# Three edits to the first pass of a fused decoder block on one core: zero matmuls ahead of the inputs, the residual of half the inputs by identity matmuls, the value tile last

## What is computed

```python
w = (qw.astype(jnp.float32) - ZERO) * jnp.repeat(scales, GS, axis=0)   # groups of 128 channels
q, k, v = x @ w_q, x @ w_k, x @ w_v          # 32 query heads, 8 key and value heads, 128 wide
q, k = _apply_rope(q, cos, sin), _apply_rope(k, cos, sin)
attn = jax.nn.softmax(causal(q @ k.T / math.sqrt(HD)), axis=-1)
x = _layernorm(x + (attn @ v) @ w_o)
...
x = _layernorm(x + _L0_xattn_ref(x, ctx_4096, ...))
x = _layernorm(x + _L0_ffn_ref(x, ...))
```

## Time and profile before

| | us |
|---|---|
| time, median of 3 runs | 696.7 (695.96 to 698.34) |
| the profiled execution's own time | 701.41 |
| its span, first to last instruction | 699.6 |
| PE busy in the span | 641.2 (92%) |
| DVE busy | 561.9 (80%) |
| ACT busy | 463.5 (66%) |
| POOL busy | 421.1 (60%) |
| mean granted clock of PE | 0.976 of full speed |

### The profile page before, as it was taken

How to read it: one execution, slowest core, us unless ns; L and a number is a source line. 1 busy time by engine, 2 the same in 40 slices (tenths; PEclk the granted TensorE clock), 3 DMA queues, 4 the chain that set the end, 5 groups by cost and what they waited for, 6 DMA issues and landing times.

```text
span 699.6 us, 10934 instructions
## 1 busy us (share of the span) xinstructions
PE 641.2 (92%) x3271; PEld 449.2 (64%) x3272; DVE 561.9 (80%) x883; ACT 463.5 (66%) x1266; POOL 421.1 (60%) x370
## 2 busy tenths in 40 slices
PE   6588989999999999999999999999878998968994
PEld 4366767768778777787777877855544444457551
DVE  4967978989999999998899999963552968997446
ACT  5377959769798797887977979865624555523000
POOL 1558779889989989988998998871221000012002
PEclk9889999999999999999999999999989999999998
DMA  6564732341351252243234224230010000020003
GB/s 208 154 207 119 235 107 60 106 130 40 93 162 37 66 155 77 46 138 103 55 112 126 48 62 134 63 114 0 1 60 1 2 0 1 1 95 2 0 1 120
DMA packets 29611, 56.72 MB, mean 81 GB/s; under 512 B 4720, under 2 KB 4976, under 8 KB 29040
## 3 DMA queue, kind: packets, MB, share of 16 engines
q1 hardware_dynamic: 29552, 56.02, 28.2%
HBM read 32.93 MB, written 2.10 MB: 50 GB/s over the span
## 4 chain that ended last, share of the span: by engine, by line
PE 39%; DVE 8%; ACT 3%; POOL 2%; issue 2%; POOLq 0%; DVEq 0%; ACTq 0%
PE ps L1507 8%; PE ps L1446 8%; PE ps L1499 7%; PE ps L1725 4%; PE ps L1461 3%; PE ps L1487 3%; DVE arena L1305 2%; PE ps L1471 1%; ACT arena L959 1%; PE ps L1607 1%; DVE arena L1278 1%; DVE late L1272 1%; DVE w_area L1286 1%; PE ps L1716 1%; DVE y L1226 1%
## 5 line engine op out<-in xcount | busy, mean ns | idle before, releaser
L1074 DVE SCALAR_TENSOR_TENSOR arena<-ps,arena 128x512 f32<-128x512 f32 x288 | 212.7, 745 | 17.5 <-PE ps L1446 4.7
L1446 PE MATMUL ps<-x_hi,w_sb 128*128 128x512 f32 x384 | 175.3, 457 | 17.0 <-DVE arena L1074 8.1
L1446 PE MATMUL ps<-x_lo,w_sb 128*128 128x512 f32 x384 | 154.6, 403 | 0.0
L1102 DVE SCALAR_TENSOR_TENSOR y<-ps,arena,y 128x512 f32<-128x512 f32 x192 | 138.8, 744 | 14.9 <-PE ps L1499 10.7
L1499 PE MATMUL ps<-heads_hi,wo_sb 128*128 128x512 f32 x256 | 110.0, 430 | 6.9 <-DVE y L1102 5.3
L772 ACT ACTIVATE arena<-ps,small 128x128 f32<-128x128 f32 x256 | 90.9, 379 | 32.3 <-DVE small L1080 32.3
L597 POOL TENSOR_TENSOR arena<-arena,consts 128x512 f32<-128x512 f32 x75 | 97.0, 1293 | 22.8 <-DVE arena L1074 22.5
L603 POOL TENSOR_TENSOR arena<-arena,consts 128x512 f32<-128x512 f32 x75 | 96.9, 1292 | 20.6 <-DMA arena<-arena 19.2
L1446 PEld LDWEIGHTS ps<-x_hi,w_sb 128*128 128x128 f32 x384 | 74.5, 194 | 51.5 <-issue 11.2
L621 POOL TENSOR_TENSOR y<-arena,y 128x512 f32<-128x512 f32 x64 | 82.5, 1290 | 40.7 <-ACT arena L813 38.6
L1499 PE MATMUL ps<-heads_lo,wo_sb 128*128 128x512 f32 x256 | 101.8, 398 | 0.0
(11 more groups left out here) (130 smaller groups left out, 957.5 us busy)
## 6 DMA issues: line engine op xcount, KB each, us to landing
arena<-arena SPq DMA_DIRECT2D x160, 128.0 KB, 2.3
arena<-in_qkv SPq DMA_DIRECT2D x48, 256.0 KB, 4.1
arena<-in_o SPq DMA_DIRECT2D x32, 256.0 KB, 3.8
arena<-in_x_t SPq DMA_DIRECT2D x8, 256.0 KB, 3.5
y<-in_x SPq DMA_DIRECT2D x4, 512.0 KB, 4.4
arena<-in_ctx_t SPq DMA_DIRECT2D x4, 512.0 KB, 6.4
out<-y SPq DMA_DIRECT2D x8, 256.0 KB, 2.2
arena<-in_wk SPq DMA_DIRECT2D x1, 1024.0 KB, 5.0
```

What stands on the lines that cost most here:

```text
L1074: nc.vector.scalar_tensor_tensor(acc, group_bank(p, KC * c + g), scale_of(p // 2, c, g), acc, ALU.mult, ALU.add).then_inc(dve_scaled, 1)
L1102: nc.vector.scalar_tensor_tensor(dst, by_tile(out_bank(p, u)), out_scale_of(p // 2, u), dst, ALU.mult, ALU.add).then_inc(out_added, 1)
L1446: mm = nc.tensor.matmul(group_bank(p, u), w_sb[:, c, g, :], part[:, g, half * HALF:(half + 1) * HALF], start=(k == 0), stop=(k == 1))
```

## The change

- DVE's first instruction sets `mask_b` to zero, and PE multiplies it by itself eight times into bank 6 while it has no inputs (`stay_busy(8)`), and twice more ahead of group 0.3.
- The weight tiles are loaded, projected and summed in the order 0, 2, 3, 4, 5, 1 (`FIRST_TILES`). Six banks instead of seven hold the groups of pass 0, since bank 6 is used for the zeros and, with bank 5, for the new cuts. `place` gives a tile's position in the new order to all waits.
- `x_lo` of the second half is no longer made by DVE. PE makes it in PSUM as identity times the piece (in full float32) plus minus identity times `x_hi` (`cut_x` of PE), and ACT copies it to `x_lo` (`copy_x_lo`). PE does the four cuts after all 24 groups of pass 0, then `turn_v(0)`, which now waits for the last copy.
- SP: the two transfers of tile 2's turn stand between the second and the third piece of the second half. POOL: the cosine of tile 2 stands ahead of the sine of tile 0.
- In phase 0 alone, PE does `score(0)` ahead of groups 1.0 and 1.1, and DVE the first maximum ahead of the sum of 1.1.

```diff
+FIRST_TILES = [0, 2, 3, 4, 5, 1]
+FIRST_SUMS = "0.1 0.2 2.1 0.3 2.2 3.1 2.3 3.2 4.1 3.3 4.2 5.1 4.3 5.2 1.1 5.3 1.2 1.3".split()
...
-        first_ps = [0, 1, 2, 7, 3, 4, 6]
+        first_ps = [0, 1, 2, 7, 3, 4]
...
+        def x_cut_bank(g):
+
+            return banks[6 if g % 2 == 0 else 5]
...
             turn_first(0)
-            for g in range(KC):
-                load_x(1, g)
-            for c in ROPE_TILES[1:]:
+            load_x(1, 0)
+            load_x(1, 1)
+            turn_first(2)
+            load_x(1, 2)
+            load_x(1, 3)
+            for c in ROPE_TILES[2:]:
                 turn_first(c)
...
+            def copy_x_lo(g):
+                act.wait_ge(x_cut, g + 1)
+                nc.scalar.activation(x_lo[:, g, HALF:], x_cut_bank(g), ACT.Copy).then_inc(x_lo_ready, 1)
+
+            first_weights(2)
             scale_group(0, 0)
-            first_weights(2)
-            scale_group(0, 1)
-            act.wait_ge(consts_in, 16)
-            nc.scalar.activation(ident_b[:, :], ident, ACT.Copy).then_inc(mask_ready, 1)
             first_weights(3)
             scale_group(0, 2)
             first_weights(4)
+            act.wait_ge(consts_in, 16)
+            nc.scalar.activation(minus_ident[:, :], ident, ACT.Copy, scale=-1.0).then_inc(mask_ready, 1)
             scale_group(0, 3)
             first_weights(5)
+            nc.scalar.activation(ident_b[:, :], ident, ACT.Copy).then_inc(mask_ready, 1)
+            scale_group(0, 4)
+            first_weights(1)
+            cut_x(1, 0)
+            scale_group(0, 5)
+            cut_x(1, 1)
+            scale_group(0, 1)
+            cut_x(1, 2)
+            copy_x_lo(0)
+            cut_x(1, 3)
+            copy_x_lo(1)
+            nc.scalar.activation(mask_b[:, :, :], mask.unsqueeze(1).broadcast_to([P, QPK, P]), ACT.Copy).then_inc(mask_ready, 1)
+            copy_x_lo(2)
+            copy_x_lo(3)
             copy_v(0)
...
+            nc.vector.memset(mask_b[:, :, :], 0.0).then_inc(idle_ready, 1)
             for g in range(KC):
                 cut_x(0, g)
...
-            for name in FIRST_SUMS[:13]:
+            for name in FIRST_SUMS:
                 first_sum(name)
-            cut_x(1, 0)
-            first_sum("4.2")
-            first_sum("5.1")
-            cut_x(1, 1)
-            first_sum("4.3")
-            first_sum("5.2")
-            cut_x(1, 2)
-            first_sum("5.3")
             first_sin(3)
-            cut_x(1, 3)
             first_total(3)
...
             def turn_v(p):
                 wait(pe, dve_scaled, summed_count(p, 1))
                 wait_turn_bank(p - 1, "V")
+                if p == 0:
+                    wait(pe, x_lo_ready, 2 * KC)
...
                 groups(0, 3)
+                if f == 0:
+                    score(0)
                 groups(1, 0, 1)
-                score(0)
+                if f != 0:
+                    score(0)
...
-            for c in range(4):
+            def stay_busy(count):
+
+                for _ in range(count):
+                    nc.tensor.matmul(banks[6], mask_b[:, 0, :], mask_b[:, :, :].rearrange("p h k -> p (h k)"),
+                                     start=True, stop=True)
+
+            def cut_x(g):
+
+                pe.wait_ge(x_hi_ready, KC + g + 1)
+                wait(pe, x_lo_ready, KC + g - 1)
+                part = slice(HALF, T)
+                nc.tensor.matmul(x_cut_bank(g), ident, x_stage[:, g, part], start=True, stop=False)
+                nc.tensor.matmul(x_cut_bank(g), minus_ident[:, :], x_hi[:, g, part], start=False, stop=True).then_inc(x_cut, 1)
+
+            pe.wait_ge(idle_ready, 1)
+            stay_busy(8)
+            for g in range(3):
+                project(0, 0, g)
+            stay_busy(2)
+            project(0, 0, 3)
+            for c in FIRST_TILES[1:]:
                 for g in range(KC):
                     project(0, c, g)
             pe.wait_ge(consts_in, 16)
+            pe.wait_ge(mask_ready, 2)
+            for g in range(KC):
+                cut_x(g)
             turn_v(0)
-            for c in range(4, NT):
-                for g in range(KC):
-                    project(0, c, g)
-            pe.wait_ge(mask_ready, 2)
+            pe.wait_ge(mask_ready, 3)
             for f in range(LAST):
                 phase(f)
```

More of the change, by code:

```diff
@@ L376, in summed_count, with place, first_bank @@
             return scaled_count(p, c, KC - 1)
+        def place(p, c):
+            return FIRST_TILES.index(c) if p == 0 else c
         def product_bank(name):
             return product_ps[PRODUCTS.index(name) % 4]
+        def first_bank(u):
+            return first_ps[(KC * place(0, u // KC) + u % KC) % len(first_ps)]
         def group_bank(p, u):
             if p == 0:
-                return banks[first_ps[u % len(first_ps)]]
+                return banks[first_bank(u)]
             return product_bank(f"G{u}")
@@ L393, in wait_group_read @@
             if u % KC == 0:
-                wait(eng, act_scaled, NT * p + u // KC + 1)
+                wait(eng, act_scaled, NT * p + place(p, u // KC) + 1)
             else:
@@ L418, in wait_product_bank @@
             if f == -1:
-                u = int(name[1:]) - len(first_ps)
-                if u >= 0:
-                    wait_group_read(nc.tensor, 0, u)
+                u = int(name[1:])
+                before = KC * place(0, u // KC) + u % KC - len(first_ps)
+                if before >= 0:
+                    wait_group_read(nc.tensor, 0, KC * FIRST_TILES[before // KC] + before % KC)
                 return
@@ L439, in wait_product_bank @@
             bank = (0, 1, 2, 7)[PRODUCTS.index(name) % 4]
-            wait_group_read(nc.tensor, 0, max(u for u in range(GROUPS) if first_ps[u % len(first_ps)] == bank))
+            places = [KC * c + g for c in FIRST_TILES for g in range(KC)]
+            wait_group_read(nc.tensor, 0, [u for u in places if first_bank(u) == bank][-1])
         def att_bank(b):
             return banks[6 if b % 2 == 0 else 4]
+        def x_cut_bank(g):
+            return banks[6 if g % 2 == 0 else 5]
         def turn_y_bank(b):
@@ L494, in _ @@
             sp.dma_start(scales[:, :], t["qkv_scales"]).then_inc(scales_in, 16)
-            load_first_w(1)
             load_first_w(2)
+            load_first_w(3)
             sp.dma_start(consts[:, :, :], t["consts"]).then_inc(consts_in, 16)
-            for c in range(3, NT):
+            for c in FIRST_TILES[3:]:
                 load_first_w(c)
@@ L759, in scale_group @@
             def scale_group(p, c):
-                wait(act, group_done, GROUPS * p + KC * c + 1)
+                wait(act, group_done, GROUPS * p + KC * place(p, c) + 1)
                 wait_ring(act, p, c)
@@ L1066, in add_group @@
             def add_group(p, c, g):
-                wait(dve, group_done, GROUPS * p + KC * c + g + 1)
+                wait(dve, group_done, GROUPS * p + KC * place(p, c) + g + 1)
                 if g == 1:
-                    wait(dve, act_scaled, NT * p + c + 1)
+                    wait(dve, act_scaled, NT * p + place(p, c) + 1)
                 else:
@@ L1438, in project @@
                 if p % 2 == 0 and g == 0:
-                    wait(pe, w_ready, NT * (p // 2) + c + 1)
+                    wait(pe, w_ready, NT * (p // 2) + place(p, c) + 1)
                 if p < 2 and c == 0:
```

19 lines of the change are left out of this document (8 added, 11 removed).

## The result

| | before | after |
|---|---|---|
| time, median of 13 runs | 698.45 (695.96 to 701.49) | 692.06 (689.33 to 695.39) |
| ratio after/before, 95% interval | | 0.9907 (0.9887 to 0.9928) |
| profiled execution, its span | 701.41, 699.6 | 692.16, 690.4 |
| mean granted clock in it | 0.976 | 0.986 |

The change makes the kernel faster by 6.5 us, with 5.0 to 7.9 as the interval. By the medians alone the difference is 6.4. The two profiled spans differ by more, 9.2, since the profiled execution of before lay 3.0 above the median of its kernel.

A forecast was written before the change was run, and what follows sets the result against it. DVE's list, from 10.35 to 33.91 us, was taken to bound the first pass. An exponential 6.9 us earlier plus 0.3 for the clock gave 7.2, so 696.7 - 7.2 = 689.5 us, range 687.2 to 693.7.

The forecast's parts named there:

- term 1: First pass: the cuts leave DVE's list, removing 4.6 us; the rotation ends at 28.9 against 33.91, 5.0 earlier.
- the sum: Whole kernel: 6.9 us from the earlier first exponential plus 0.3 from phase 0's clock, 7.2 us gained.
- rivals 1 and 2: Start: cuts gate phase 0, 691.7 to 693.7 us, chance 0.14; or zeros don't raise the clock, 691.3, chance 0.13.
- The body moves rigidly: Attention phases behind the first 64 us: each waits only on the one before, so early gains or losses move all behind.
- The collision: First pass: one DVE rotation operation meets POOL on the shared port pair, at most 1.28 us, taken as 0.2.
- Term 2: Start on PE: zero matmuls let the clock rise between 4 and 11 us; little gain, already in the 28.9.
- The walk: First pass: DVE's new order stepped through with row durations; ends at 28.9, 1.5 to 2 us later if the clock rises at 14.7.
- rival 2: Start on PE: zeros don't raise the clock, exponential at 34.2, gain 5.4, time 691.3 us; chance 0.13.
- Term 3: End of first pass: cuts on PE and ACT cost 1.08 each, 4.3 in all; phase 0 starts at 28.0, cover 1 us.
- Rival 4: Cuts ahead of the scores: slower, if a cut on PE costs about 3.6 us instead of 1.08; chance 0.04.
- Term 4: Phase 0: scores go ahead of groups 1.0 and 1.1; first exponential at 32.7 against 39.58, 6.9 us earlier.
- Term 5: Phase 0's clock on PE: the second half-clock dip may come again, move or vanish, 0 to 1.7 us, taken as 0.3.

The follow-up runs named there:

- e0: The changed kernel run again without any edit, on the chip of the next three runs: 692.37 us, ratio 0.9902 to the kernel before.
- v1: The changed kernel with all four x pieces of the second half issued ahead of the first turn: 691.41 us, ratio 0.9886 to the kernel before.
- e3: The changed kernel with the four cuts of the second half back on DVE; zeros, tile order and score order kept: 696.61 us, ratio 0.9977 to before.
- e5: The changed kernel with the sine and total of tile 5 moved from DVE to POOL: 692.54 us, ratio 0.9926 to the kernel before.
- x1: The changed kernel with each cut's float32 identity matmul done twice on PE: 696.74 us, ratio 0.9966 to the kernel before.
- e1: The changed kernel without the zero matmuls and the memset: 692.86 us, ratio 0.9914 to the kernel before.
- e2: The changed kernel with phase 0's scores and first maximum back behind groups 1.0 and 1.1: 692.70 us, ratio 0.9916 to the kernel before.
- e4: The changed kernel without zeros and with the scores in their old place, on a second chip: 694.14 us, ratio 0.9930 to the kernel before.
- b2: The kernel before plus 18 filler matmuls in PE's idle time between phase 0's groups: 696.47 us, ratio 0.9987 (0.9960 to 1.0014).
- b1: The kernel before plus only the memset and the ten zero matmuls: 698.63 us, ratio 0.9996 to the kernel before.
- v3: The changed kernel with early x pieces and phase 0's first maximum one sum earlier on DVE: 691.84 us, ratio 0.9907 to the kernel before.
- v2: The changed kernel with early x pieces and without the zero matmuls: 693.62 us, ratio 0.9908 to the kernel before.

## Why the prediction was right

The forecast was faster, by the mechanism of term 1, and its case came true; the measured difference is 6.4 where the sum said 7.2. The time alone would not have shown that: 692.06 is nearer to what rivals 1 and 2 gave (691.7 to 693.7, and 691.3) than to 689.5. What decides between them is the trace, where the rotation, the cuts and phase 0's start are where the forecast had them, and the level (last point). By its steps:

- **The body moves rigidly: right within the noise.** PE's busy time in it changed by 0.3. The last column of the table spreads over 3.9 us, and between the profiles of before and after the shift of the scores goes from 7.7 (phase 1) over 7.0 (phase 2) to 8.8 (phase 10). Why was not followed.
- **Term 1: right, its exactness partly luck.** The rotation's end was put at 28.9 and came at 28.99, but two misses cancel in it: DVE's first sum came at 9.60 instead of 10.35, and the list from there took 19.39 instead of 18.55. In e0 the rotation ended 0.7 later. The x piece was to land at 17.7 and ACT started on it at 17.49; DVE's wait for it was 1.15, put at 0.8. The collision was put at 0.2 and cost 0.95 - 0.68 = 0.27, in e0 0.14, in v1 0.75. The exclusion of DVE and POOL was argued from two rows; e3 and e5 show it, in both directions and with other operations. The rule of the Trainium skill named there (SBUF — State Buffer, "Who interferes with whom") holds in both.
- **Term 2: the clock rose at 5.0, inside the forecast's 4 to 11, but the rest was overrated.** The walk had the exponential 1.5 to 2 us later with a rise at 14.7. Without zeros it came at 32.70, between the two profiles with them (32.09, 32.94), and the time was 0.5 to 0.8 longer. Part of it is that the clock rose at 12.5 there, not at 14.7. The sign was right, the price some 1 us too high. That is also where rival 2 ended: zeros do count, and it would hardly have mattered had they not.
- **Term 3: the sizes were right, the cover was wrong.** 1.09 per cut against 1.08, the last copy ended at 26.9 against 27.4, phase 0 started at 27.43 against 28.0. But the text set phase 0's start on PE (28.0) against the rotation's end on DVE (28.9) and called the difference a cover of 1 us. The two lists meet later: DVE's first sum of phase 0 also needs ACT's copy of v and scaling behind that start, and the scores need the four groups. The prediction had the consequence in term 4 (sums "from about 29.5", after 28.9) and didn't draw it. In the trace ACT was done at 28.89 and DVE started its sum at 28.99. That 0.1 is no cover but the handover: in x1 the sum, which waited for ACT, also starts 0.11 behind ACT's end (32.98, 33.09). DVE by itself would have been ready 0.61 behind the start of its last total, at 28.94, so both branches end together. In e0 ACT's came 0.2 later than DVE's, in e1 and v1 it was 0.4 earlier (ACT's scaling ended at 29.15 and 28.57, the sums started at 29.62 and 29.08, less the handover). The cover is between -0.2 and 0.4, not 1. PE reached the mask at 29.58 without a wait. x1 confirms it: with 3.4 us more on the cuts, DVE's first sum of phase 0 moves by 4.1 (3.2 from e0's 29.85) and the end by 4.4.
- **Rival 4 was closer than it was made.** Its mechanism has the right place, and its point of decision used that cover. Without it, a cut has to cost 9.0 / 4 = 2.25 more, 3.3 and not 3.6. It stays far from the 1.09 measured.
- **Term 4: right in the trace, not in the time.** The exponential was put at 32.7 and came at 32.09 and 32.94. Taking the scores' move back delays it by 0.9 to 1.7, yet costs 0.3 to 0.6 in e2; from e1 to e4, where the same edit is the only difference (but the chip is another), it costs 1.3, or 1.1 by the ratios. None of these is clear of the noise. Where the rest is made up was not followed.
- **Term 5 and the sum.** The first exponential moved by 7.5 and the phase-1 scores by 7.7, so the profile agrees with 7.2. But the sum was made against the one profiled execution of before, which lay 3.0 above its median of 13, with two stretches of half clock ahead of phase 1. A gain read off it holds part of that.
- **The level.** 696.7 was the median of three runs; 13 gave 698.45. With the same difference, 691.3 would have been said, 0.8 from the result instead of 2.6. This, not the mechanism, is the larger part of the error in the predicted time.

**What stays open** is how much of the gain is DVE's time as such and how much the clock's. Within each kernel the runs' times rise with their half-clock time, by 0.32 us per us over 70 runs of before (which spend 32 us there in the median, 25 to 44) and by 0.30 over 22 runs of e0, e1 and e2. The changed kernel spends 19. (The measure leaves out the start, which has no clock record before the first rise.) Worked out from that, up to 0.3 x 13 = 4 of the 6.4 us would go with the clock: PE no longer idles between 24.5 and 34.7, so it keeps its clock there. This is a correlation. The one run that removed half-clock time and nothing else, b2, gained 2.3 in the median with an interval that includes no change. x1 speaks for the plain account: its half-clock time is that of e0 (22 us in the median of both), and it lost 4.4 against e0. In e3 it is 26, so by the same 0.3 some 1.3 of its 4.2 us would be the clock's; this is an estimate. Open too is what cuts cheaper than 1.09 would bring, since both branches now end together.

## What to carry to other kernels

Before moving work off an engine, write down for the new place what the in-order list puts between that work and the instruction that waits for both branches: cover is the difference of the two arrivals at that instruction, not at the first one behind the moved work. An idle POOL is no free capacity for elementwise work while DVE works on two SBUF operands (e5). PE's idle time while it waited for DVE took four subtractions as float32 identity matmuls, but no more than that: 3.4 us on top cost 4.4 (x1). Compare medians of a dozen runs before taking a difference from two profiles: here the profiles said 9.2 and the runs 6.4.

## What the runs showed of the hardware

- Multiplying zeros raises the clock as other work does: in b1 and in the changed kernel eight such matmuls were all that PE had done before the rises at 4.3 and 5.0. The Trainium skill (TensorE: Matmul & The Clock Gate, Part 1) says that activity releases the throttle; these runs add that multiplying zeros by zeros is such activity.
- The early rise is not certain. In the nine profiles with the zeros it came at 4.3 to 5.0 in five (after, b1, e2, e3, v1) and at 9.2 to 10.2 in four (e0, e5, v3, x1); in the five without them it came at 11.7 to 14.7 (before, b2, e1, e4, v2). After and e0 are the same instructions.
- Nor does it always last: in b1, e3 and v1 the clock fell again at 7.7, 7.7 and 8.2, for 3 to 7 us. In all three PE's starts up to there are within 0.1 us of the changed kernel's, where the clock stayed up.
- DVE's operation on two SBUF operands of 128x512 float32 takes 0.67 to 0.69 alone and 0.82 to 1.76 beside one of POOL, and POOL's 1.28 becomes 1.41 to 1.74. DVE's sums, which read PSUM and SBUF, kept their 0.70 each beside POOL (22.21 in the kernel before, beside POOL's operation at 22.02).
- A full float32 matmul of 128x512 costs 0.86 at full clock (the distance in x1), 3.7 times the 0.23 of the rounded type.
